# A sequence layer in one kernel: output tables loaded over nine pairs of frequency slots, and four moves in the order of the expert stage

## What is computed

```python
u = x @ W_in + b_in                                   # 512 -> 1536
x0, x1, v = split(short_conv3(u, short_w) + short_b)  # 3-tap convolution along the sequence
k = filter(W1, b1, f1, W2, b2, f2, W3, b3)            # small sine network, damped by exp(-t*delta)
v = irfft(rfft(pad(v * x1)) * conj(rfft(k))) + filter_bias
x = layernorm(x + (v * x0) @ W_out + b_out)

grouped = x.reshape(groups, 32, 512)                  # 256 groups of 32 rows
logits = grouped @ controller + tie                   # 32 rows x 128 (expert, set) per group
perm = (logits == max over the 32 rows)               # one row per expert and set
picked = perm^T @ grouped
inner = relu(picked @ f1 + bias)                      # 512 -> 32 per expert and set
out = perm @ (inner @ f2)                             # back to the 32 rows
x = layernorm(x + out)
```

## Time and profile before

| | |
|---|---|
| three runs, median | 2126.2 us |
| the profiled execution: its time / its span | 2126.09 us / 2123.9 us |
| PE matmul busy | 1981.5 us, 93% of the span |
| DVE, ACT, POOL busy | 1438.7, 1042.4, 437.2 us |
| mean granted TensorE clock | 0.983 of full speed |
| DMA queue of SP and ACT | 360.42 MB |
| frequency phase, first to last `transform` | 773.2 to 1115.5 us of the span |
| expert phase, first product | 1540.23 us of the span |

### The profile page before, as it was taken

One profiled execution on the slowest core, in us unless ns is written; L12 is line 12 of the kernel. 1 busy time (PEld: TensorE's weight loads), 2 busy tenths in 40 slices (PEclk: granted clock), 3 DMA queues, 4 the chain that ended last, 5 costly groups with the idle time before them and its releaser, 6 DMA issues. The chain is left out here.

```text
span 2123.9 us, 43999 instructions
## 1 busy us (share of the span) xinstructions
PE 1981.5 (93%) x16950; PEld 1462.9 (69%) x16950; DVE 1438.7 (68%) x2833; ACT 1042.4 (49%) x1875; POOL 437.2 (21%) x282
## 2 busy tenths in 40 slices
PE   7999999999999879899996999999878988889898
PEld 6777777777777634344444888888767777677685
DVE  5977877777878835454554888898754655646645
ACT  4444444444444434345443555555432844826637
POOL 0100001100001014345444555545200000000000
PEclk9999999999999989999999999999989999999999
DMA  6133433333432258788876877777367576584663
GB/s 175 65 109 110 138 115 105 119 105 114 133 121 102 100 185 220 224 222 241 231 213 183 249 247 242 245 232 244 127 221 244 160 241 207 168 298 145 199 236 120
DMA packets 228051, 380.02 MB, mean 179 GB/s; under 512 B 23647, under 2 KB 90117, under 8 KB 227717
## 3 DMA queue, kind: packets, MB, share of 16 engines
q1 hardware_dynamic: 218629, 360.42, 53.8%
q10 hardware_dynamic: 9216, 16.78, 2.1%
HBM read 251.00 MB, written 126.12 MB: 178 GB/s over the span
## 5 line engine op out<-in xcount | busy, mean ns | idle before, releaser
L90 PE MATMUL p_pu<-p_xT_high,p_win_high 128*128 128x512 f32 (+1 forms) x816 | 330.9, 405 | 14.2 <-DVE p_win_low L85 11.9
L446 ACT ACTIVATE p_t<-p_pu,p_tbias,p_taps 128x512 f32<-128x512 f32 (+1 forms) x192 | 146.7, 764 | 357.9 <-PE p_pu L92 357.0
L91 PE MATMUL p_pu<-p_xT_high,p_win_low 128*128 128x512 f32 (+1 forms) x816 | 314.1, 385 | 0.0
L92 PE MATMUL p_pu<-p_xT_low,p_win_high 128*128 128x512 f32 (+1 forms) x816 | 313.9, 385 | 0.0
L1472 DVE COPY e_taken<-e_pun 128x1024 f32<-128x1024 f32 x126 | 154.2, 1224 | 129.4 <-PE e_pun L1399 88.6
L1472 ACT COPY e_taken<-e_pun 128x1024 f32<-128x1024 f32 x122 | 123.4, 1013 | 223.1 <-PE e_pun L1399 184.1
L563 DVE SCALAR_TENSOR_TENSOR p_t<-p_pu,p_taps,p_t 128x256 f32<-128x256 f32 (+1 forms) x384 | 208.4, 543 | 6.9
L847 POOL TENSOR_TENSOR q_y<-q_y 128x512 f32<-128x512 f32 x128 | 160.3, 1271 | 195.6 <-DVE q_y L868 195.6
L85 POOL TENSOR_TENSOR p_xT_low<-p_xT,p_xT_high 128x2048 fp32r<-128x2048 f32 (+1 forms) x16 | 71.3, 4455 | 619.8 <-ACT p_xT_high L80 619.8
L90 PEld LDWEIGHTS p_pu<-p_xT_high,p_win_high 128*128 128x128 f32 x816 | 156.3, 192 | 46.7 <-DVE p_xT_low L85 10.0
L92 PEld LDWEIGHTS p_pu<-p_xT_low,p_win_high 128*128 128x128 f32 x816 | 155.7, 191 | 32.9
(11 more groups left out here) (163 smaller groups left out, 3882.9 us busy)
## 6 DMA issues: line engine op xcount, KB each, us to landing
q_av<-s_SV SPq DMA_DIRECT2D x64, 512.0 KB, 4.2
s_Z<-q_z SPq DMA_DIRECT2D x128, 256.0 KB, 3.2
o_zin<-s_Z SPq DMA_DIRECT2D x64, 512.0 KB, 3.9
e_ff<-in_L_ffn_f SPq DMA_DIRECT2D x64, 512.0 KB, 4.7
e_it<-in_L_ffn_f SPq DMA_DIRECT2D x48, 512.0 KB, 5.1
s_X<-p_t SPq DMA_DIRECT2D x64, 256.0 KB, 2.3
s_SV<-k_shared SPq DMA_DIRECT2D x64, 256.0 KB, 2.0
s_SV<-p_sout SPq DMA_DIRECT2D x64, 256.0 KB, 2.0
```

Source lines behind the costliest of these rows:

```text
L90: pe.matmul(out, a[0], b[0], start=start, stop=False)
L91: pe.matmul(out, a[1], b[0], start=False, stop=False)
L92: return pe.matmul(out, a[0], b[1], start=False, stop=stop)
L446: nc.scalar.activation(t[r][m % 2][:, c], pu[(W + n) % 3][:, c], ACT.Identity, bias=tbias[:, w:w + 1], scale=taps[:, w, 2:3]).then_inc(t_o ...
```

## The change

Five edits, all in the order of the streams; no computation is added or left out, and the stream of PE keeps its order entirely.

- Frequency phase, SP: `wout` is loaded in four quarters of 256 KB at steps 16 to 19, then one table a step at steps 20 to 24. ACT waits for all four quarters (`ONE + 16 * DT`) where it waited for the one load.
- Expert phase, SP ("late tile fetch"): the five tiles of the next chunk are issued at i = `Q - NF` = 24, behind all 32 weights of this chunk, and before the first weights of the next one.
- Expert phase, ACT ("last copies first"): the last copy of a chunk's dispatch comes before `root` and `finish` of the previous chunk's row tile.
- Expert phase, DVE (the same): the last copy comes right after `clear(c)`, and `moments` and `scale` of the previous chunk's tile follow it.
- Expert phase, DVE ("biases early"): `prepare()` runs after the third row tile of the first dispatch instead of after the last.

```diff
-                if p == PAIRS // 4:
-                    sp.dma_start(wout[:], A["W_out"].rearrange("(k p) d -> p k d", p=P)).then_inc(w_in, 16)
+                q = p - PAIRS // 4
+                if 0 <= q < DT:
+                    sp.dma_start(wout[:, q, :], A["W_out"].rearrange("(k p) d -> p k d", p=P)[:, q]).then_inc(w_in, 16)
+                if q == DT:
                     sp.dma_start(O["grow"][:], A["grow"]).then_inc(carried, 16)
+                if q == DT + 1:
                     sp.dma_start(O["grow_c"][:], A["grow_c"]).then_inc(carried, 16)
...
-                    act.wait_ge(w_in, ONE + 16)
+                    act.wait_ge(w_in, ONE + 16 * DT)
...
-                    if i + NF < Q or i + NF < Q + NO and c + 1 < CHUNKS:
+                    if i + NF < Q:
                         load_weights(n + NF)
-                    if i == Q // 2:
+                    if i == Q - NF:
                         if c + 1 < CHUNKS:
...
+                    if Q <= i + NF < Q + NO and c + 1 < CHUNKS:
+                        load_weights(n + NF)
...
+                    if c < CHUNKS and m == TC:
+                        take("send", c, 2 * m - 1)
                     if c and m >= behind:
                         root(j)
...
-                    if c < CHUNKS and m:
+                    if c < CHUNKS and 0 < m < TC:
                         take("send", c, 2 * m - 1)
...
-                    if c and m >= behind:
+                    if c and m >= behind and (m < TC or c == CHUNKS):
                         scale(j)
                     if c < CHUNKS and m:
                         take("send", c, 2 * m - 2)
+                        if c and m == TC:
+                            moments(j)
+                            scale(j)
+                        if c == 0 and m == PT - 1:
+                            prepare()
...
                         if c < CHUNKS and m == TC - 1:
                             clear(c)
-                        moments(j + 1)
+                        else:
+                            moments(j + 1)
...
                 if c == 0:
-                    prepare()
                     clear(0)
```

More of the change, by code:

```diff
@@ L729, in _ @@
                                      ).then_inc(tiles_in, 16)
-                if p == PAIRS // 4:
-                    sp.dma_start(wout[:], A["W_out"].rearrange("(k p) d -> p k d", p=P)).then_inc(w_in, 16)
+                q = p - PAIRS // 4
+                if 0 <= q < DT:
+                    sp.dma_start(wout[:, q, :], A["W_out"].rearrange("(k p) d -> p k d", p=P)[:, q]).then_inc(w_in, 16)
+                if q == DT:
                     sp.dma_start(O["grow"][:], A["grow"]).then_inc(carried, 16)
+                if q == DT + 1:
                     sp.dma_start(O["grow_c"][:], A["grow_c"]).then_inc(carried, 16)
+                if q == DT + 2:
                     sp.dma_start(O["fbias"][:], A["filter_bias"]).then_inc(carried, 16)
+                if q == DT + 3:
                     sp.dma_start(O["bout"][:], A["b_out"].rearrange("(a d) -> a d", a=1).to_broadcast([P, D])
                                  ).then_inc(carried, 16)
+                if q == DT + 4:
                     sp.dma_start(O["ctrl"][:], A["ffn_controller"].rearrange("(k p) e -> p k e", p=P)).then_inc(carried, 16)
```

## The result

The changed kernel took 2109.99 us (median of 6, 2104.76 to 2115.65) against 2126.2 for the one before, a ratio of 0.9925 [0.991, 0.9941]. Timed twice more, in later batches, it gave 2115.0 us, 0.9947 [0.9928, 0.9966], and 2117.25 us, 0.994 [0.9919, 0.9961]. The three ratios have a mean of 0.9937: the change gains some 13 us (11 to 16), not the 25 of the forecast. The profiled execution took 2112.03 us (span 2109.9, mean granted clock 0.985 where it was 0.983). Its span is 14.1 us shorter than before's, but not all of that is the edits': 2.2 us lie in the first 33 us, in the front phase, which no edit touches (granted clock 1.00 over the first 40 us, where the execution before had 0.96).

The account below looks back on a forecast made before the run. PE has work in 93% of the span, so only its standing or slow places could pay: −8.0 − 1.3 − 7.8 − 4.2 − 4.1 = −25.4 from 2126.1, predicted 2101 us; 2098 to 2104 at 55%, 2096 to 2110 about 8 in 10.

Parts of the forecast that it names:

- (a): Frequency phase, step 16: spreading the tables over nine steps removes the 8.3 us stall; −8.0 us, bounds −8.3 to −0.4.
- R3: Rival, frequency phase: each of nine pairs waits 0.88 us for its spread load; 2108 us, chance 8%.
- R4: Rival, frequency phase: spread loads saturate the queue and every pair loses time, slower than before; 2175 us, chance 2%.
- R5: Rival, frequency phase: the stall at step 16 only moves, so the table edit gains nothing; 2109 us, chance 4%.
- a granted clock of 1.00 from 780 to the phase's end: Sign for (a), frequency phase: full clock from 780 us on, beside no `q_pv` wait above 0.5 us near step 16.
- (c): Later chunks' starts: last copies first cuts PE's idles of 3.81, 4.09 and 3.81 us to near 1.3; −7.8 us.
- the clock term: First 128 expert products of each chunk: clock stays up after shorter stops; −4.2 us, bounds −5 and 0.
- (d): Expert steps: the late tile fetch removes PE's three waits for weights; −4.1 us, bounds 0 and −6.
- (b): First chunk's start: early `prepare` saves 2.0 us of PE's wait, less 0.7 of slip; −1.3 us, bounds −2.0 to 0.
- the `issue` row still near 15 us: Sign for (d), expert steps: PE's `issue` gaps stay near 15 us; growth above 4 us would make the prediction wrong.
- R2: Rival, expert steps: weights and `issue` gaps take back fetch, clock and some of (c); 2112 us, half way 2106, chance 18%.
- R1: Rival, chunk starts: the clock still falls, so (b) and (c) keep only the idle time; 2105 us, chance 10%.

Follow-up runs that it names:

- e9: Changed kernel with each of the three 640 KB tile-point loads cut into three DMAs on three steps in a row; 2108.77 us, ratio 0.9916.
- e3: Kernel before with the late tile fetch alone; ratio 0.9981 [0.997, 0.9992], −4.0 us.
- e1: Kernel before with the tables spread over nine steps alone; ratio 0.995 [0.9938, 0.9963], −10.6 us.
- e12: Kernel before with the early preparation alone; 2129.28 us, ratio 1.0005 [0.9989, 1.002].
- e8: Changed kernel with the last two of the four weight loads at a chunk's stop held until PE ends the second step's first products; 2110.41 us, ratio 0.9925.
- e10: Changed kernel with e8, e9, preparation before DVE's second copy and bias loads after the second row tile; 2104.22 us, ratio 0.9888.
- e2: Kernel before with last copies first alone; ratio 0.9953 [0.9941, 0.9964], −10.0 us.
- e4: Changed kernel without the late tile fetch; ratio 0.9944 [0.9927, 0.9961], −11.9 us against the kernel before.
- e6: Changed kernel loading only half of each weight block from the ninth expert step on; 2087.63 us, ratio 0.9809 [0.9783, 0.9834].

## Why the prediction was wrong

**(a) right.** −8.0 forecast, −8.3 against before in every trace that has it, no wait at any of the nine steps, clock 1.00 there. R3, R4 and R5 did not happen. The cost that I put at 0.3 us was not seen; the waits at the three tile points vary as much without the edit, and e9 shows that they are avoidable. The sign of "a granted clock of 1.00 from 780 to the phase's end" failed in the profile, at 1117 us, for 1.4 us.

**(c)'s own term right.** −7.8 forecast, 2.46 + 2.74 + 2.46 = −7.66, the same within 0.01 us per stop in all eleven traces that have it, released by DVE's copy as foreseen. What it leaves out is what comes behind the stop, under the clock term.

**(d) nearly right alone.** −4.1 forecast, −4.0 [−6.4, −1.7] measured in e3. On top of (c) it seems to be worth less, though the spread is as large as the difference: the stretches of chunks 1 to 3 have a mean of 189.2 us with both and 191.7 with (c) alone, 2.5 us, out of five and three traces.

**(b) wrong.** Forecast −1.3, and 0.9 more for the clock. The stop did shrink to 2.06 us, but the same time went in at 1546.25, the start of the steps moved by only 0.8 us, and the first code block took more than that back; alone the edit measures 1.0005 [0.9989, 1.002], an interval that holds −1.3 too, so it is the trace that shows the miss. The step that failed is the sentence that the copy "now begins about 1.7 us later" at a price of 0.7: I priced what DVE would lose, but not that PE's next products wait for exactly this copy.

**The clock term failed, and with it the forecast.** It said −4.2 us. The observation was right in three chunks of the profile: after 1.35 us of standing the 128 products take 2.56 us, not 3.62. The inference was not: that PE's time saved there is the kernel's. The code block lands as late as before, and PE, there 1 us sooner, waits for it. The sum had put the `issue` gaps at unchanged ("the `issue` row still near 15 us"); with (c) PE's waits in chunks 1 to 3 rose from 17.0 us to 20.9. It is R2's mechanism, which I gave 18% and priced at 2112 us. Forecast for chunks 1 to 3 were 3.3 us of clock and 4.1 of fetch off the stretches, 7.4 in all; the five traces with both have a mean of 189.2 us, the three with neither (before, e1, e12) one of 188.4. By the means that makes about 8 us, to which (b) and the clock of chunk 0 add 2 to 4, an estimate that would account for the distance from 25 to 13; the means are good to about 2 us each, so the split is not shown. R2 named weights and `issue` gaps together. It was the gaps: the time came back as the wait for code, which in the changed kernel's chunk 2 started on its way 5.6 us after the first product and, with half of the burst held back (e8), 2.7 us after it.

**R1 in part.** In chunk 0 the clock fell after the stop of 2.06 us (3.29 us for 124 products), though in the earlier trace rows it had stayed at 1.00 over a stop of 2.24; in e10 it stayed over one of 1.98, and fell 5.6 us after the first product. Nor did it always stay up over the stop of 1.35 us: the first 124 products took 2.3 us or less in most chunks, but 3.1 and 3.2 in chunk 1 of e2 and e4 and 3.2 in chunks 2 and 3 of e6. The Trainium skill, "TensorE: Matmul & The Clock Gate", section "Part 1: The HAM clock gate", says that the place of the change varies between runs; these traces agree with that.

What stays open: single executions differ by 3 us and more either way, and the gaps behind the first block wander between the code places; why one execution has a gap of 3.5 us at a block where another has none is not settled. Nor is it why the three edits, measured alone, gave 24.6 us with intervals of about 2.5 each, when in the traces (c) alone returns as much as it does beside (a); e2's trace is at −6.4 us (span 2117.5) while its median is at −8.2, so part of the surplus may be the draw. And how much of the 12 us between forecast and result each of the three wrong steps took is known only by the estimate above.

## What to carry to other kernels

Where an engine's code comes through the same DMA engines as its data, what a shorter stop in front of a burst of loads wins can be waited out in part at the next code block (here 3.9 us in three chunks, beside 7.7 us of shorter stops that stayed won): look for waits without a releaser at fixed distances behind the stop, and hold a part of the burst back or thin it. A load put between an engine's regular transfers should be cut to one piece per period, and then checked at every place where several still stand together. When pricing an operation moved to an earlier place in a queue, price what the other engine waits for behind it, not only what its own queue loses.

## What was not expected of the hardware

- Code blocks: 138 packets of 16 KB in the span, each about 1.0 us on its way once started; PE went on 0.9 to 1.7 us after one had landed; with weights at full size it waited 18 to 31 us for them in the expert steps, with half the bytes 4.9 and 5.0 us.
- The place of the first block's wait is fixed by the code, its length by the load: behind product 231 of chunk 2 it was nothing in four traces without (c), and 1.0 to 2.6 us in eight with it (in e8, with half of the burst held back, nothing).
- The granted clock fell also deep in the steps, after gaps of 1.9 us and more in some executions, and not after a gap of 1.51 or a stop of 1.35 us in the changed kernel's trace, though after the same stop of 1.35 us in four chunks of e2, e4 and e6.
